# A mixer that opens in an order of its own, with PSUM banks for its second batch, and the seams before and behind it

## What is computed

```python
h = _layernorm(x, axis=-1) * (1 + ca) + sa
x = x + ga * _L1_attn_ref(h, ...)      # linear attention: qf = elu(q)+1, kf = elu(k)+1
#   kv = einsum(kf, v); out = (qf @ kv) / (qf . sum(kf)); out @ wo.T + bo
h = _layernorm(x, axis=-1) * (1 + cb) + sb
x = x + gb * _L1_ffn_ref(h, ...)
#   src = rmsnorm(h + gqa(h));  src = src + moe(src);  rmsnorm(src)
#   moe: top 2 of 8 experts, 256 -> 512 -> gelu -> 256, a capacity for each expert
```

## Time and profile before

| | us |
|---|---|
| runs of the kernel before | 3208.58, 3211.11, 3212.12 (median 3211.11) |
| the profiled execution | 3202.91 |
| its span in the trace | 3201.2 |
| TensorE busy in the span | 3019.7 (94%) |
| VectorE busy | 2199.2 (69%) |
| ScalarE busy | 1560.5 (49%) |
| GpSimd busy | 1206.1 (38%) |

### The profile page before, as it was taken

One profiled execution on the slowest core, in us unless ns is written; L12 is line 12 of the kernel. 1 busy time (PEld: TensorE's weight loads), 2 busy tenths in 40 slices (PEclk: granted clock), 3 DMA queues, 4 the chain that ended last, 5 costly groups with the idle time before them and its releaser, 6 DMA issues. The chain is left out here.

```text
span 3201.2 us, 58149 instructions
## 1 busy us (share of the span) xinstructions
PE 3019.7 (94%) x19352; PEld 1857.1 (58%) x19352; DVE 2199.2 (69%) x6730; ACT 1560.5 (49%) x3524; POOL 1206.1 (38%) x1521
## 2 busy tenths in 40 slices
PE   6799999999998996899999999999999968999996
PEld 3566766666665774344444444444444327888886
DVE  6777777777763333778888888888888852445545
ACT  3466556565652112466666666666666641111111
POOL 2123223232234212333444444444443243455454
PEclk8899999999999998899999999999999989999998
DMA  8111111010122981222222222222222207899995
GB/s 290 7 38 59 33 64 33 33 64 33 43 91 90 319 285 36 67 60 62 75 72 71 74 77 77 77 77 77 77 77 73 80 33 214 241 276 275 274 268 159
DMA packets 291043, 354.72 MB, mean 111 GB/s; under 512 B 49856, under 2 KB 240563, under 8 KB 290753
## 3 DMA queue, kind: packets, MB, share of 16 engines
q1 hardware_dynamic: 261760, 313.28, 31.1%
q0 software_dynamic: 28464, 34.71, 5.1%
q10 hardware_dynamic: 544, 3.15, 0.3%
HBM read 234.02 MB, written 122.34 MB: 111 GB/s over the span
## 5 line engine op out<-in xcount | busy, mean ns | idle before, releaser
L2861 DVE TENSOR_REDUCE negmax<-psum 128x1 f32<-128x512 f32 x1024 | 669.2, 684 | 123.1 <-PE psum L3435 119.3
L2490 ACT ACTIVATE pT<-psum 128x512 f32<-128x512 f32 x1024 | 576.9, 600 | 255.6 <-PE psum L3461 221.5
L3435 PE MATMUL psum<-k_stack,q_stack 96*128 96x512 bf16 x1024 | 355.5, 387 | 11.3 <-DVE negmax L2861 8.2
L3461 PE MATMUL psum<-q_stack,k_stack 99*128 99x512 bf16 x1024 | 347.5, 381 | 9.4 <-ACT pT L2490 6.2
L4061 POOL DMA_INDIRECT src_rows<-ye,place x142 | 222.4, 1566 | 282.0 <-DVE ye L4113 228.7
L964 ACT ACTIVATE probs<-probs,negmax 128x256 f32<-128x256 f32 x512 | 252.8, 495 | 124.1 <-DVE negmax L1055 122.5
L4078 ACT ACTIVATE actT_x<-psum 128x512 f32<-128x512 f32 x142 | 84.8, 597 | 438.9 <-PE psum L4203 438.9
L3475 PE MATMUL psum<-pT,v_tile 128*32 128x512 f32 x2048 | 272.5, 604 | 1.6 <-ACT pT L2490 1.0
L4203 PE MATMUL psum<-xT_x,w_x 128*128 128x256 f32 x1136 | 257.9, 381 | 0.0
L4215 PE MATMUL psum<-w_x,actT_x 128*128 128x256 f32 x1136 | 256.6, 379 | 0.0
L1055 DVE CUSTOM_DVE_ANT_0 probs<-psum,band_mask 128x256 f32<-128x256 f32 x512 | 181.4, 420 | 104.3 <-PE psum L1329 103.9
(11 more groups left out here) (409 smaller groups left out, 5619.4 us busy)
## 6 DMA issues: line engine op xcount, KB each, us to landing
w_x<-in_L_ffn_w_dram SPq DMA_DIRECT2D x142, 512.0 KB, 5.4
w_e<-in_L_ffn_w_dram SPq DMA_DIRECT2D x46, 1024.0 KB, 6.3
q_stacks<-q_part SPq DMA_DIRECT2D x192, 128.0 KB
q_stack<-q_stacks SPq DMA_DIRECT2D x64, 384.0 KB, 3.8
padded<-w_e SPq DMA_DIRECT2D x32, 650.0 KB, 6.1
...
```

The costliest lines, as they stand in the source:

```text
L2490: act.activation(pT[:, 4 * (s % 2) + r, :], bank(m, 2 + n % 2), ACT.Exp, scale=float(DHQ) ** -0.5)\
L2861: dve.tensor_reduce(negmax[:, p // REP, h:h + 1], bank(m, max_bank(b, 16 * g + p)), AX.X, ALU.max, negate=True).then_inc(max_read, 1)
L3435: pe.matmul(bank(m, max_bank(b, 16 * g + p)), q_stack[0:K_SCORE, h, t * P:(t + 1) * P], k_stack[0:K_SCORE, g, :], start=True, stop=True).t ...
L3461: pe.matmul(bank(m, 2 + n % 2), k_stack[:, g, kc * P:(kc + 1) * P], q_stack[:, REP * g + r, :], start=True, stop=True).then_inc(sT_done, 1)
```

## The change

1. In the first layer's experts the norm for the mixer is cut in three: the statistics behind tile 14, the root behind tile 16, and the rows themselves ahead of the last tile's `copy_out`.
2. The mixer's start is one hand-written order on each engine, `opening()`, in the place of partial bodies and `entry()`. On GpSimd the key sums stand ahead of the query sums; on ScalarE and VectorE the roots stand elsewhere. Batch 1 has banks of its own (`SECOND`), and most of its waits on a bank are gone. `max_scores` of batch 0 goes over two banks from the first on. `keep_busy` is left out ahead of batch 1's product L3348.
3. For batch 15 `transpose_o2`, `project2` and `transpose_src` start on the row tiles that are there. The constants of the lists stand ahead of body(16). `keep_busy` at the end has three products.
4. GpSimd no longer waits for the last scatters at the mixer's end. In the next block SyncE issues three weight loads first, then waits for the scatters, then loads rows. TensorE's `up(0)` stands ahead of `transpose(1)`, and `root` behind `copy_out`.
5. The last batch's norm works in two halves, with the first guess of each root from ScalarE and one step of refinement in the place of three, and SyncE holds back the stores of batch 14 until the last rows have been loaded.

```diff
@@ routed experts, VectorE
-            def mixer_norm():
-                step = Steps(dve, m.norm0_s, (B + NG) * LN_STEPS, LN_STEPS)
-                emit_layernorm(dve, step, m, [...], m.xn0_ready, None, all_rows_read)
+            def mixer_stats():
+                for t in range(NT):
+                    norm(dve.bn_stats(m.bn[:, t, :], batch[t]))
+            def mixer_root():
+                norm.settle()
+                for t in range(NT):
+                    norm(dve.bn_aggr(m.meanvar[:, t, :], m.bn[:, t, :]))
+                norm.settle()
+                emit_rsqrt(dve, norm, m, m.rstd[:, 0:NT], m.meanvar[:, 0:NT, 1], LN_EPS, NT)
+            def mixer_rows():
+                dve.wait_ge(xT_done, NTILE0)
+                for t in range(NT):
+                    dve.tensor_scalar(m.xn[:, t, :], batch[t], ..., ALU.subtract, ALU.mult)
...
+                if i == NTILE0 - 1:
+                    mixer_rows()
                 copy_out(i)
-                if i == NTILE0 - 2:
-                    mixer_norm()
+                if i == 14:
+                    mixer_stats()
+                if i == 16:
+                    mixer_root()
@@ mixer: banks
+        SECOND = dict(hidden=(5, 0), query=(1, 2), key_value=(3, 5, 0, 1), numerator=(2, 3, 5, 2), o1=(3, 5), project1=(5, 5))
...
-            return bank(m, FIRST[product][i] if is_first(b) else LB)
+            return bank(m, FIRST[product][i] if b == 0 else SECOND[product][i] if b == 1 else LB)
...
-            return n % 4 if is_first(b) and n < 24 else n % 2
+            return n % 2
@@ mixer: SyncE
-            def entry():
+            def opening():
+                load_rows(0)
+                store_first(0)
                 store_keys(0)
                 load_stack(0, 0)
+                load_rows(1)
                 load_stack(0, 1)
                 max_rows(0, 0)
                 load_h2_rows(0)
                 store_second(0)
-                load_rows(2)
                 load_stack(0, 2)
                 load_stack(0, 3)
+                load_rows(2)
                 max_rows(0, 1)
                 store_first(1)
@@ mixer: GpSimd
-            pool.wait_ge(scattered, B * (NT * TOPK * 16))
-            take_wait(pool, m)
-            pool.wait_ge(src_out, B * 16)
@@ mixer: ScalarE, the start of its order
+            def opening():
+                modulate(0, 0)
+                first_seed(1)
+                modulate(0, 1)
...
                 modulate(1, 0)
                 modulate(1, 1)
-                query_parts(1, 0)
                 second_seed(0, 0)
...
@@ mixer: VectorE, the part before batch 0's scores (opening() and entry() were two lists)
+                first_newton(1)
                 add_experts(0)
...
-                first_newton(1)
                 add_experts(1)
...
                 cut_max(0, 0)
+                row_max(0, 1, 0)
                 divide(1, 2)
                 divide(1, 3)
-                row_max(0, 1, 0)
                 row_max(0, 1, 1)
+                first_newton(2)
...
             for b in range(0, B + 3):
+                if b == B:
+                    list_constants()
                 body(b, b % 2, lambda k: 0 <= b + k < B)
@@ mixer: TensorE
             def key_values_sum(b):
-                if b < 2:
+                if is_first(b):
                     keep_busy(pe, m, 0, 2)
...
             def transpose_o2(b, j):
                 if j == 0:
+                    pe.wait_ge(o2_ready, b * NT + (2 if is_last(b) else NT))
+                elif is_last(b):
                     pe.wait_ge(o2_ready, b * NT + NT)
...
             def project2(b, j):
                 if j == 0:
+                    pe.wait_ge(o2T_ready, b * 2 + (1 if is_last(b) else 2))
+                elif is_last(b):
                     pe.wait_ge(o2T_ready, b * 2 + 2)
...
                 for t in range(NT):
+                    if c == 0 and is_last(b):
+                        pe.wait_ge(src_ready, b * NT + t + 1)
...
-            keep_busy(pe, m, 3, 8)
+            keep_busy(pe, m, 3, 3)
@@ experts of the second layer: SyncE
-            for i in range(WB):
-                load_rows(i)
+            for i in range(2):
                 e = number(i, E - 1)
                 load_up(i, e)
-                load_down(i, e)
+                if i == 0:
+                    load_down(i, e)
+            sp.wait_ge(m.scattered, B * (NT * TOPK * 16))
+            load_rows(0)
+            load_rows(1)
+            load_down(1, e)
+            e = number(2, E - 1)
+            load_up(2, e)
+            load_down(2, e)
+            load_rows(2)
...
             for h in range(2):
+                sp.wait_ge(src_in[h], 16 * TOPK * (B // 2 + 1 - h))
+            for h in range(2):
                 store(B - 2, h)
@@ GpSimd, ScalarE
+            pool.wait_ge(m.src_out, B * 16)
...
+            act.preload_act_table_set("natural_log_exp_and_others")
+            for h in range(2):
+                half = m.rstd[:, 2 * h:2 * h + 2]
+                act.wait_ge(norm_s, last_variance[h])
+                act.activation(half, m.var_eps[:, 2 * h:2 * h + 2], ACT.Ln).then_inc(gelu_ready, 1)
+                act.wait_ge(gelu_ready, 2 * NTILEX + 2 * h + 1)
+                act.activation(half, half, ACT.Exp, scale=-0.5).then_inc(gelu_ready, 1)
@@ VectorE
-                if i >= 14 and i % 4 == 2:
-                    root()
...
                 copy_out(i)
+                if i >= 14 and i % 4 == 2:
+                    root()
...
-                for t in (2 * h, 2 * h + 1):
-                    step(dve.bn_stats(m.bn[:, t, :], src[:, (B - 1) % 2, 0, t, :]))
-            root()
-            dve.wait_ge(x_ready, 2 * (B - 1))
+                last_stats(h)
             for h in range(2):
+                last_root(h)
                 for t in (2 * h, 2 * h + 1):
                     scale(B - 1, t, step)
+                if h == 0:
+                    dve.wait_ge(x_ready, 2 * (B - 1))
@@ TensorE
             transpose(0)
+            up(0)
             transpose(1)
-            up(0)
```

245 lines of the change are left out of this document (154 added, 91 removed).

## The result

The changed kernel took 3185.87 us (median of five runs, 3184.11 to 3195.60) where the kernel before took 3212.12 beside it (3208.58 to 3215.40): a ratio of 0.9923, with an interval of 0.9907 to 0.9940, 26.3 us less by the medians. Forecast were 3186.9 us and a ratio of 0.9925. On a second occasion it took 3183.29 (3181.47 to 3184.58) beside 3206.85, ratio 0.9926 (0.9912 to 0.9940), 23.6 us less.

The account below looks back on a forecast made before the run. TensorE bounds the bodies, so gains come at the seams: norm 7.0, opening 12.4, mixer's end 1.4, next block 1.0, end 2.4, together 24.2 us off the median 3211.11, giving 3186.9 us (range 3179 to 3197).

Parts of the forecast that it names:

- (b): Opening, key sums first on GpSimd: keys' product starts at 1244.9 instead of 1246.85, divisions 3 us earlier.
- (c): Opening, VectorE: sums of expert rows start earlier with less company, so the gates end at 1258.7, 4.4 us earlier.
- (d): Opening, GpSimd: batch 1's norm is over early and the branch's sum follows each gate, ending 5.7 us earlier.
- (e): Opening: with ScalarE's seed in front the second norm starts at 1262.8, not 1273.03; first store 11.9 us earlier.
- (f): Opening: the landing of the stack's load decides the first scores, which come at 1289.9, 12.3 us earlier.
- (g): Opening: sixteen maxima over two banks instead of four take 1.5 us longer (0 to 3).
- (h): Opening: scoresT no longer waits for 24 maxima and comes 7.6 us behind the sixteenth, instead of 9.1.
- (a): Opening, ScalarE: the first seed ahead of the second `modulate` makes the queries start 0.8 us late.
- "Opening pays half": Rival: in the opening a link taken as free holds, giving 3193.1 us; chance 0.17.
- The rule weighed in (c): Opening: VectorE and GpSimd instructions exclude each other on SBUF for a whole instruction; gates 1.2 us later, total gain 1.2 smaller.
- "rows behind weights": Rival, next block: the opening's rows land after the weights, losing 2 us instead of gaining 1; 3189.9 us, chance 0.12.
- "Slower": Rival, bodies: VectorE stalls beside GpSimd sums; 1.7 us per body eats everything, 3 us gives 3231.9; chance 0.03.

Follow-up runs that it names:

- `after_again`: The changed kernel without any edit, profiled a second time; this execution took 3182.05 us.
- `key_bank`: The changed kernel with one shared PSUM bank for the second batch's four key and value products; one execution, 3184.48 us.
- `opening_only`: The kernel before with only the opening's new order and banks, and the list constants ahead of body(16); ratio 0.9971 to before.
- `root_late`: The changed kernel with VectorE's root steps of the second batch moved back behind the four divisions; one execution, 3189.01 us.
- `no_hold`: The changed kernel without SyncE's two waits that hold back the stores of the fifteenth batch; one execution, 3188.04 us.
- `rows_again`: `rows_first` unchanged, measured again beside `rows_bridge`; 3186.55 us, ratio 0.9921 to before.
- `rows_bridge`: `rows_first` with 12 idle products ahead of the next block's first transposes and 5 ahead of its first up; 3182.87 us, ratio 0.9911 to before.
- `busy_block`: The changed kernel with 20 idle TensorE products at the start of the second layer's experts; median 3183.29 us.
- `rows_first`: The changed kernel with SyncE waiting for the scatters first, then loading each tile's rows ahead of its weights; 3180.18 us, ratio 0.9923 to before.

## Why the prediction was right, and where it was not

**The total.** 3186.9 us forecast, 3185.87 measured, and the mechanism of each seam but the next block's was found where it was put. That the two stand only 1 us apart is luck: for a forecast of 24.2 us, the medians give 26.3 and 23.6, by the intervals of their ratios anything from 19 to 30, and single executions give 20.9 and 22.9. That the same 24.2 may be taken off the median, 8.2 us above the execution it was worked from, held within this. The changed kernel's profiled execution stood 9.2 us over its own median, so such a distance belongs to an execution; in the changed kernel the stages with a lower clock show it, for the 3211 us of before no trace does.

**The norm in pieces.** Mechanism and size right at the seam: 1.01 us of wait and 3.72 for 6.33 and 5.40, the first row 5.0 and 7.4 us earlier for 7.0. The first of them has 1.8 us in two waits of TensorE for rows of other tiles, which `after_again` does not have. In the whole time the part alone measured 4.2, between 1.3 and 7.4; the term is right as a stage and uncertain as a total.

**The opening,** step by step, in us behind the mixer's first row:

| | before | forecast | after |
|---|---|---|---|
| (b) keys' product starts, and takes | 20.4, 3.56 | 18.5, 2.6 | 18.8, 2.04 |
| (c) gates end | 36.7 | 32.3 | 33.9 |
| (d) branch's sum ends | 39.5 | 33.9 | 35.5 |
| (e) second norm starts | 46.6 | 36.4 | 38.2 |
| (f) first store; stack's load; first scores | 58.7; 70.2; 75.8 | 46.8; 58.3; 63.5 | 47.6; 59.2; 64.1 |
| (g) sixteenth maximum ends | 86.5 | 75.7 | 76.0 |
| (h) first scoresT | 95.7 | 83.3 | 83.9 |

(a) holds: the queries 0.75 us late for 0.8. In (c) I let the gates follow VectorE's own sums, but they wait for TensorE (1.30 us), whose `project1` products ran at half the clock, 5.41 us; that is the 1.6 us too little, carried through (d) and (e) and half made good by the queries, which I had made the bound of the store. In (f) "the landing decides" is right, and the banks are what makes it so: with one bank TensorE came 2.1 us behind the landing (`key_bank`).

The sums of (e) and (f) are also 0.4 us short each: 1264.2 + 10.7 - 2.5 + 1.2 is 1273.6 and not 1273.2, and 5.6 us behind the load at 1284.7 is 1290.3 and not 1289.9; with both the gain comes to 11.6. (g) measured 1.8 for 1.5, with thirteen maxima in 9.05 us, 0.70 each. "Opening pays half" is refuted for the seam by both executions and by `opening_only`; its gain of 12.4 is 11.8 against the execution that it was worked from, and 9.4 against the other, in which before kept more of its clock. That is the term's real fault: part of what I counted as waits removed was one execution's clock.

The rule weighed in (c) forecast 1.2 us of interference; the first sum took 0.94 for 0.69, so 0.25. And the row that it was weighed on says more than the rule: the small VectorE instruction of 8.53 us stood beside a dozen GpSimd sums of 0.7 us one after the other, not beside one, so "the trace agrees" holds for the interference and not for its length.

**The mixer's end.** Near the 1.4 in one pair, 1.2 us up to batch 15's logits (23.50 in `after_again` for 24.66), and none of it later. It is not shown apart from the clock, which was at half for the last 4.3 us of that stage in `after_again` and for 5.5 in before; `root_late`, `no_hold`, `rows_again` and `rows_bridge`, with this part in, took 24.7 to 24.8 us, of which 6.5 to 6.8 at half. The wait for `src` lost 0.9 of its 5.62 us. GpSimd's last scatter starts 16.5 to 17.1 us behind those logits, for 16.5, and what the list's constants cost is not shown.

**The next block.** This step failed: a loss of 1.4 to 2.7 us, counted from the start of GpSimd's last scatter to the third up (26.8 and 28.1 us for 25.4; 26.8 to 28.4 in five executions with this order for 25.4 to 25.9 in four with that of before), in the place of a gain of 1.0. Two parts of it were mis-sized. "2.7 us earlier" for the meeting was 0.9: the first record of the next block, a table load on ScalarE at 2636.42 in after, stands 2.3 us behind the recorded end of GpSimd's last scatter, which I had taken for the end of its work. And the rows, which I thought to come with `up(0)` as the bound, came 5.08 us behind their issue for 2.8; and with 12.43 us without work ahead of it `up(0)` ran 6.73 and 5.33 us for 4.59 (3.72 in `busy_block`, which fills that time). This is the rival "rows behind weights" at 0.12, at its own price of 2, and `rows_first` shows it by undoing it: 3.5 us. The Trainium skill, DMA: Bandwidth & Descriptors, "Queues, rings and completion order", says that descriptors are taken in the order of the ring and that the signal lands behind all earlier writes of its engine; the trace agrees with late rows, 2.3 us of them, and I should have given it more than a tenth, with three weight loads written out ahead of the rows.

**The end.** 3.0 us for 2.4 (stage 532.15 for 535.11). The scatter: last issue 3.90 us behind TensorE's end for 4.88, 1.0 for the 0.5. The stores held back: 0.2 to 0.7 for the 0.9. The halves: 5.75 us from the second half's sum to the last one for 6.94, 1.2 for the 1.0. "Slower" had no sign in any trace: TensorE idled 1.4% in the bodies of after for 1.3%. "Nothing comes of the opening" is refuted by `opening_only`.
